# Gated attention stage: the projection ahead of the maxima chunk in each unit, at most two chunks to a unit, and the expert ranks one operation at a time

## The reference, cut to what matters

```
B, T, DIM = (4, 1024, 128);  H, E, DH, K = (8, 5, 64, 3)
ss = sigmoid(x @ Ws).reshape(b, t, H, E);  sd = sigmoid(x @ Wd).reshape(b, t, H, E)
ms, md = topk_mask(ss, K), topk_mask(sd, K)          # 3 of 5 experts stay
q5 = (x @ Wq).reshape(b, t, H, E, DH)                # k5, v5 alike, from Wkv
q = einsum('bthed,bthe->bhtd', q5, sd * md)          # k, v with ss * ms
attn = softmax(einsum('bhid,bhjd->bhij', q * DH**-0.5, k))
out = einsum('bhij,bhjd->bihd', attn, v)
o5 = (out @ Wo).reshape(b, t, H, E, DIM)
y = einsum('bthem,bthe->btm', o5, md)
x = layernorm(x + y)
```

## Time and profile before

| what | value |
|---|---|
| median of three runs | 4347.36 us (4346.91 to 4350.75) |
| the profiled execution's own time | 4350.9 us |
| its span in the profile | 4349.2 us |
| gated stage, unit 0 of group 0 to the end of group 15's products | 1280 to 2529 us |
| mean granted TensorE clock over the span | 0.955 |
| busy shares of the span | PE 89%, DVE 75%, POOL 68%, ACT 44% |

### The profile page before, as it was taken

One profiled execution on the slowest core, in us unless ns is written; L12 is line 12 of the kernel. 1 busy time (PEld: TensorE's weight loads), 2 busy tenths in 40 slices (PEclk: granted clock), 3 DMA queues, 4 the chain that ended last, 5 costly groups with the idle time before them and its releaser, 6 DMA issues. The chain is left out here.

```text
span 4349.2 us, 63343 instructions
## 1 busy us (share of the span) xinstructions
PE 3864.7 (89%) x22554; PEld 2205.7 (51%) x22554; DVE 3243.0 (75%) x5670; ACT 1925.3 (44%) x3478; POOL 2938.9 (68%) x2166
## 2 busy tenths in 40 slices
PE   7999999999788889899899848999999999999964
PEld 4555555555455555555555424555455444545533
DVE  6876878868487777877876648887888788878826
ACT  3443444434355455455455313444444444434423
POOL 3776767667536777877787835777677677767740
PEclk8999999999889999999999968999999999999987
DMA  3000100000010000100100021221222121212121
GB/s 55 21 22 1 38 14 25 10 6 1 27 59 20 28 19 28 38 19 28 33 28 10 6 59 30 41 34 30 39 32 43 30 40 30 43 22 44 19 59 30
DMA packets 98073, 125.90 MB, mean 29 GB/s; under 512 B 28928, under 2 KB 76480, under 8 KB 97760
## 3 DMA queue, kind: packets, MB, share of 16 engines
q1 hardware_dynamic: 97760, 121.86, 13.2%
HBM read 103.69 MB, written 18.12 MB: 28 GB/s over the span
## 5 line engine op out<-in xcount | busy, mean ns | idle before, releaser
L845 POOL TENSOR_TENSOR s_psum_p<-s_psum_p,s_prob 128x1024 f32<-128x1024 f32 (+3 forms) x640 | 1336.9, 2089 | 387.0 <-ACT s_prob L550 336.7
L550 ACT ACTIVATE s_prob<-s_sT 128x1024 f32<-128x1024 f32 (+2 forms) x896 | 792.0, 931 | 842.9 <-DVE s_sT L701 474.1
L449 PE MATMUL s_pv<-s_prob,s_vp 128*64 128x512 f32 (+3 forms) x3584 | 798.9, 567 | 3.9 <-POOL s_prob L830 3.9
L657 DVE CUSTOM_DVE_ANT_0 s_mx<-s_mx,s_strip 128x512 f32<-128x512 f32 x628 | 422.0, 714 | 161.8 <-PE s_mx L406 159.1
L1734 POOL TENSOR_TENSOR s_psum_p<-s_psum_p,s_prob 128x1024 f32<-128x1024 f32 x192 | 462.1, 2407 | 108.0 <-ACT s_prob L1457 106.2
L1457 ACT ACTIVATE s_prob<-s_sT 128x1024 f32<-128x1024 f32 x256 | 262.7, 1026 | 581.5 <-PE s_sT L1321 581.4
L706 DVE RECIPROCAL s_recip<-s_recip 128x128 f32<-128x128 f32 x512 | 452.7, 922 | 34.8 <-ACT s_recip L497 34.8
L406 PE MATMUL s_mx<-s_bh,s_ah 64*128 64x512 f32 (+2 forms) x1756 | 396.7, 447 | 87.2 <-DVE s_bm L647 39.0
L845 POOL TENSOR_TENSOR s_psum_p<-s_prob 128x1024 f32<-128x1024 f32 (+1 forms) x128 | 288.1, 2251 | 204.7 <-ACT s_prob L550 202.0
L449 PEld LDWEIGHTS s_pv<-s_prob,s_vp 128*64 128x64 f32 x3584 | 219.3, 137 | 369.0 <-issue 289.2
L647 DVE TENSOR_REDUCE s_bm<-s_mx 128x6 f32<-128x768 f32 (+2 forms) x376 | 360.0, 957 | 53.3 <-PE s_mx L406 44.6
(11 more groups left out here) (291 smaller groups left out, 7418.7 us busy)
## 6 DMA issues: line engine op xcount, KB each, us to landing
s_strip<-bias_rows SPq DMA_DIRECT2D x256, 144.0 KB, 5.8
s_wr<-gated_weights SPq DMA_DIRECT2D x32, 960.0 KB, 4.9
s_near<-bias_rows SPq DMA_DIRECT2D x256, 48.0 KB, 2.0
x<-s_x SPq DMA_DIRECT2D x10, 512.0 KB, 3.2
s_x<-x SPq DMA_DIRECT2D x8, 512.0 KB, 4.7
gated_weights<-s_side_hi SPq DMA_DIRECT2D x8, 480.0 KB, 2.6
gated_weights<-s_side_lo SPq DMA_DIRECT2D x8, 480.0 KB, 2.9
s_x<-in_L_attn_x_dram SPq DMA_DIRECT2D x4, 512.0 KB, 5.4
```

What stands on the lines that cost most here:

```text
L449: last = mm(pv[heads(hd), lo:CH], vp[:, g % 2, j, heads(hd)], prob[:, k % PR, hd, lo:CH], start=j == 0, stop=end)
L550: nc.scalar.activation(prob[:, k % PR, :, lo:CH], sT[:, k % 2, :, lo:CH], ACT.Exp, scale=st.scale).then_inc(exp_done, 1)
L657: last = nc.vector.tensor_tensor_reduce(out=mx[:, hd, :], in0=mx[:, hd, :], in1=strip[:, g % 2, hd, first:first + CH], scale=1.0, scalar=N ...
L845: nc.gpsimd.tensor_tensor(out[:, :, lo:CH], src, p[:, :, lo:CH], ALU.add)\
```

## The change: what it does

- In each unit PE, and DVE with it, take the projection steps first and the first maxima chunk after them. Before, the chunk came first.
- `mx_steps` becomes one chunk in units 4 to 9 and two in each of units 10 to 14. All go to the bank pair `mx`; the second of a unit still follows the values product.
- `mt_unit` becomes 15, and the transpose stands right behind that unit's scores, ahead of its small jobs and values. `max_rows` stands first on DVE in unit 15.
- Of the products "zp" for blocks 0 to 3 the places become units 13, 14, 15, 15 (before: 12, 13, 14, 15).
- "gx" and "gl" move from units 6 to 9 to units 12 to 15 of groups 0, 3, 7. The rank operations, before in clusters of three (units 10, 11 and 14 of those groups, and 8, 9 and 11 of groups 1, 4, 8), all move to units 0 to 11 of groups 1, 4, 8, one or two at a time. Only a different cutting of the same 20 instructions is made.
- The layer norm's steps 0 and 1 move from units 13 and 14 to unit 15, steps 2 to 5 from unit 15 and units 2, 3, 6 to units 4, 5, 6, 6, step 6 from 7 to 9.

```diff
@@ class Gated @@
-        self.mx_steps = [0] * 4 + [1] * 6 + [2, 2, 3, 3, 0, 0]
+        self.mt_unit = 15
+        self.mx_steps = [0] * 4 + [1] * 6 + [2] * 5 + [0]
...
-        for i in range(4):
-            out[12 + i].append(("zp", g, i))
+        for i, u in enumerate((13, 14, 15, 15)):
+            out[u].append(("zp", g, i))
...
-            for u, job in ((6, ("gx", gated, 0)), (7, ("gx", gated, 1)), (8, ("gl", gated, 0)),
-                           (9, ("gl", gated, 1)), (10, ("top", gated, 0)), (11, ("top", gated, 1)),
-                           (14, ("top", gated, 2))):
+            for u, job in ((12, ("gx", gated, 0)), (13, ("gx", gated, 1)), (14, ("gl", gated, 0)),
+                           (15, ("gl", gated, 1))):
...
-            for k, u in enumerate((8, 9, 11)):
-                out[u].append(("top", ranked, 3 + k))
+            for n, u in enumerate((0, 0, 1, 2, 3, 4, 4, 5, 5, 6, 6, 7, 7, 8, 9, 11)):
+                out[u].append(("top", ranked, n))
...
-        for n, (of, u) in enumerate(((1, 13), (1, 14), (1, 15), (2, 2), (2, 3), (2, 6), (2, 7))):
+        for n, (of, u) in enumerate(((1, 15), (1, 15), (2, 4), (2, 5), (2, 6), (2, 6), (2, 9))):
@@ PE's loop over the units @@
-                early = 1 if steps else 2
-                for t in chunks[:early]:
-                    maxima(t[1], t[2], second(todo, t, k))
+                early = 1
+                if ("mt", g + 1) in todo:
+                    m_transpose(g + 1)
                 for n, t in enumerate(steps):
                     project(t[1], t[2], k if n == 0 else None)
+                for t in chunks[:early]:
+                    maxima(t[1], t[2])
...
                 for t in chunks[early:]:
                     maxima(t[1], t[2])
-                if ("mt", g + 1) in todo:
-                    m_transpose(g + 1)
@@ DVE's loop over the units @@
-                early = chunks[:1] if steps else chunks[:2]
-                for t in early:
-                    maxima(t[1], t[2], second(todo, t, k))
+                early = chunks[:1]
+                if ("mt", g + 1) in todo:
+                    max_rows(g + 1)
                 for n, t in enumerate(steps):
                     project(t[1], t[2], k if n == 0 else None)
+                for t in early:
+                    maxima(t[1], t[2])
```

More of the change, by code:

```diff
@@ L54 @@
 RINGP = 5
-TOPS, TOPC = E0 + 1, 8 + 3 * (E0 - 1)
+TOPS, TOPC = 4 + 3 * (E0 - 1), 8 + 3 * (E0 - 1)
 class Pairs:
@@ L1576, in x_lo, with top_experts @@
                 tt(xl[:, half(c)], xT[:, half(c)], f32(xh[:, half(c)]), ALU.subtract).then_inc(xl_done, 1)
-            def top_experts(b, k):
+            def top_experts(b, n):
                 gates, kept = gate[:, b % 2, :, :], keep[:, :, :]
-                at = TOPC * b + E0 + 3 * (k - 1)
-                if k == 0:
+                k, part = divmod(n + 2, 3)
+                if n == 0:
                     dve.wait_ge(sig_done, 2 * b + 2)
@@ L1585, in top_experts @@
                         nc.vector.memset(kept[:, e, :], float(E0 - 1 - e)).then_inc(top_step, 1)
-                elif k < E0:
+                    return
+                dve.wait_ge(top_step, TOPC * b + E0 + n - 1)
+                if k < E0:
                     later, earlier, won = slice(k, E0), slice(0, E0 - k), beats[:, 0:E0 - k, :]
-                    dve.wait_ge(top_step, at)
-                    tt(won, gates[:, earlier, :], gates[:, later, :], ALU.is_ge).then_inc(top_step, 1)
-                    dve.wait_ge(top_step, at + 1)
-                    tt(kept[:, later, :], kept[:, later, :], won, ALU.add).then_inc(top_step, 1)
-                    dve.wait_ge(top_step, at + 2)
-                    tt(kept[:, earlier, :], kept[:, earlier, :], won, ALU.subtract).then_inc(top_step, 1)
-                else:
-                    dve.wait_ge(top_step, at)
-                    nc.vector.tensor_scalar(kept, kept, float(TOP) - 0.5, None, ALU.is_lt)\
-                        .then_inc(top_step, 1)
-                    dve.wait_ge(top_step, at + 1)
-                    tt(gates, gates, kept, ALU.mult).then_inc(top_step, 1)
+                    if part == 0:
+                        ins = tt(won, gates[:, earlier, :], gates[:, later, :], ALU.is_ge)
+                    elif part == 1:
+                        ins = tt(kept[:, later, :], kept[:, later, :], won, ALU.add)
+                    else:
+                        ins = tt(kept[:, earlier, :], kept[:, earlier, :], won, ALU.subtract)
+                elif part == 0:
+                    ins = nc.vector.tensor_scalar(kept, kept, float(TOP) - 0.5, None, ALU.is_lt)
+                elif part == 1:
+                    ins = tt(gates, gates, kept, ALU.mult)
+                else:
                     if b >= 2:
                         dve.wait_ge(share_done, 2 * NP * (b - 1))
-                    nc.vector.tensor_copy(
+                    ins = nc.vector.tensor_copy(
                         keep_d[:, b % 2, :, :, :],
-                        kept.rearrange("p e (i s h) -> p e i s h", i=NB, s=2)[:, :, :, 1, :])\
-                        .then_inc(top_step, 1)
+                        kept.rearrange("p e (i s h) -> p e i s h", i=NB, s=2)[:, :, :, 1, :])
+                ins.then_inc(top_step, 1)
+                if n == TOPS - 1:
                     dve.wait_ge(top_step, TOPC * (b + 1))
@@ L1696, in _ @@
                             head_maxima(t[1])
-                    elif t[0] == "mt":
-                        max_rows(t[1])
                     elif t[0] == "ln":
```

## The result

The changed kernel took 4379.28 us in the median of five runs (4377.75 to 4382.35), the kernel before, on the same chip, 4348.33 us (4346.91 to 4362.53). The ratio of the two kernels over all these runs is 1.0066, with a 95% interval from 1.0053 to 1.0080: slower by some 29 us (the medians are 31 us apart), where +12 us, 4359 us, had been forecast.

What follows compares the result with a forecast made beforehand. PE was taken to bound the stage, with stalls at bank reads, chunk reductions and rank operations. Terms -15 + 16 + 20 + 19 - 40 - 2 + 14 = +12 on 4347.4 gave 4359 us, range 4328 to 4380.

Steps and rivals of the forecast that it cites:

- the ranks stay dear: Rival: rank operations meet POOL additions as often in their new places, saving only 22 us; 4377 us, chance 0.16.
- term A: Units 4, 6, 7, 8, 9: projection first shortens each period by 0.22 us, -15 us in all.
- term D: Unit 0 of the next group: late products meet POOL additions, so PE waits up to 1.85 us; +19 us.
- term G: Granted clock: the 13 new unit 0 waits bring ten falls of 1.4 us each; +14 us.
- term E: Ranking groups: rank operations spread out remove 40 of their 45.4 us excess over plain groups; -40 us.
- F: Layer norm steps and xs in their new places, against their cost in groups 6 and 10; -2 us.
- term B: Units 10 and 11: the first chunk's reduction stands behind DVE's pieces, units take 6.4 and 6.65 us; +16 us.
- C: Units 12 to 15: all chunks in mx, two turns a unit, and a later transpose lengthen them; +20 us.
- unit 0 doesn't wait: Rival: the late products escape POOL's additions, so unit 0's wait and most clock falls are gone; 4326 us, chance 0.24.
- The waits come, the clock holds: Rival: unit 0 waits as forecast but no clock falls follow; 4345 us, chance 0.20.

Runs made afterwards that it cites:

- run 2: Kernel before with only the new places of the rank operations, gx, gl and layer norm steps: 4304.74 us, ratio 0.9878.
- run 6: The whole change, with the softmax-sum products over 64 columns of ones instead of one: 4361.68 us, ratio 1.0024.
- run 2b: The same kernel as run 2, measured again on another chip: 4307.55 us, ratio 0.9899.
- 3: Kernel before with only at most two chunks a unit, all in mx, transpose in unit 15, products in units 13, 14, 15, 15: 4386.21 us, ratio 1.0061.
- 9: Kernel before with the new rank, gx, gl and layer norm places, and projection first only in units 6 to 9: 4300.36 us, ratio 0.9883.
- 9b: The same kernel as 9, measured again: 4299.69 us, ratio 0.9880.
- 1: Kernel before with only the projection ahead of the chunk in the one-chunk units, 4 to 9: 4356.33 us, ratio 1.0004.
- 4: Kernel before with new rank, gx, gl and layer norm places, and projection first in units 4 to 9: 4308.17 us, ratio 0.9889.
- run 5: The whole change, with the zp products of blocks 0 to 3 moved earlier, to units 12, 12, 13, 14: 4373.02 us, ratio 1.0049.
- Run 11: Kernel before with new rank and layer norm places, projection first in units 10 and 11 too, three chunks kept in units 12 and 13: 4342.45 us, ratio 0.9974.
- 7: Kernel before with new rank and layer norm places, projection first in units 4 to 9, softmax sums over 64 columns: 4304.20 us, ratio 0.9891.
- run 12: Kernel before with new rank and layer norm places, projection first only in units 6 to 9, softmax sums over 64 columns: 4302.26 us, ratio 0.9889.

## Why the forecast was right, and where not

The sign and nearly every unit time held. The range held by luck as much as by reason: 4379.28 us lies 0.7 us inside its upper end, 4380, and outside the 4350 to 4370 that the forecast had for itself. The number nearest to the result, 4377, belonged to the rival that the ranks stay dear, which the runs rule out. The sum, +12, missed the +29 of the ratio by 17 us. Two more errors cancel: term A gained 8 us less than forecast, and term D cost 7 us less. What is left of the miss is nearly all in term G. Term by term, the change against the mean of both profiles of run 2 for all but E and F (table of groups 0 to 13; where falls blur a term, run 6's row, which has the fewest, stands in):

| term | forecast | measured | from |
|---|---|---|---|
| A, projection first | -15 | -7 | run 6: units 6-9 -10.3, units 4-5 +3.6 |
| B, units 10 and 11 | +16 | +15.9, one fall in it | 181.0 against 165.1 |
| C, units 12 to 15 | +20 | +23.6, four falls in it | run 6: 223.2 against 199.6 |
| D, unit 0 | +19 | +12 | 95.3 against 83.3 |
| E and F, ranks, layer norm | -42 | -40 | run 2 against before |
| G, clock | +14 | about +28 | what is left of +28.2 in groups 0 to 13, with C at 19; 22 falls at 1.33 us, from run 6, are 29 |

In the last line the four falls are taken out of C at a good 1 us each, as in unit 12 of the change, 4.82 us with a fall and 3.8 without one. Groups 14 and 15, which the sum had left out, took 107.8 us to the start of their last unit, against 101.8; two profiles of one kernel, runs 2 and 2b, differ there by 3.0 us, so I give no cause for those 6.

**Term G is the step that failed.** The sum let the clock fall only behind the waits of term D: "The 13 new waits of term D would bring ten" falls. Seven of the waits came in full (unit 0 of 7.2 to 8.9 us), and three falls followed. In before, eight of ten such waits had one behind them (two of the ten are in group 14, whose units have no projections, so that six of eight is what the rows give for groups 0 to 13). And in the change there were 22 falls in groups 0 to 13: eleven in units 5 and 6, seven in unit 12, three in unit 1 and one in unit 11. What the sum had left at nothing, or in its upper bound alone, were two other places.

The larger one is units 5 and 6. No wait stands ahead of these eleven falls. In groups 1 to 13 of the change PE has no idle time at all in units 4 and 5, where it had some 0.4 us or more in unit 4 before. Run 6 has as little idle time there and no such fall, so that alone isn't it. Two things go with these falls, in groups 0 to 13:

| unit 5 | profiles | falls in units 5 and 6 |
|---|---|---|
| chunk first, one-column sums | before, 2, 2b, 3, 9, 9b | 1, 0, 1, 0, 0, 0 |
| projection first, one-column sums | the change, 1, 4, 5, 11 | 11, 7, 3, 7, 8 |
| projection first, sums of 64 columns | 6, 7 | 0, 0 |

With both the new order of unit 5 and the one-column products there are 36 falls in five profiles. Where either is missing (run 12, with neither, has none) there are two in nine. The smaller place is unit 12: four of its seven falls (groups 2, 3, 7 and 11) begin behind the new wait of 1.8 us in unit 11, which term B brings and for which the sum had no fall. In run 6, with the same waits, groups 3 and 11 still have theirs.

The price was right: 16 falls fewer made run 6 21.3 us shorter than the change in groups 0 to 13, 1.33 us for each, where 1.4 was taken. The counting was wrong in a second way. Nine of the eleven falls of before began in the six groups with rank operations, and with the ranks' new places run 2 has none in all and run 2b one; the cost of the nine was already in the 45.4 us excess that term E cut from. So nearly all 22 had to be counted as new, not 11 more than before.

**Term A** is right in units 6 to 9 (0.19 us a unit, 0.22 forecast; unit 7 of groups 5, 9 and 13 lost 0.4), half right in unit 4 (4.67 against 4.79 us), and wrong in a sentence that was not priced: "Units 0 to 3 and 5 are full of PE work." Unit 5 is, and there the order costs, 5.94 against 5.55 us. The rows of PE in unit 5, group 11, before:

```profile
2205.97 0.43 PE L1321 MATMUL s_sT<-s_mr,s_rowsel 64*128 64x512 f32 x2
2206.20 0.42 PE L1286 MATMUL s_mx<-s_bh,s_ah 64*128 64x512 f32 x2
2206.55 0.47 PE L1254 MATMUL s_sT<-s_wr,s_xh 128*128 128x448 f32 x1
...
2207.74 0.39 PE L1256 MATMUL s_sT<-s_wr,s_xh 128*128 128x512 f32 x1
2207.97 1.84 PE L1181 MATMUL s_misc<-constants,s_psum_p 128*128 128x1 f32 x16
2209.74 1.08 PE L1333 MATMUL s_pv<-s_prob,s_qkv 128*64 128x512 f32 x4
```

And after:

```profile
2219.04 0.40 PE L1321 MATMUL s_sT<-s_mr,s_rowsel 64*128 64x512 f32 x2
2219.37 0.47 PE L1254 MATMUL s_sT<-s_wr,s_xh 128*128 128x448 f32 x1
...
2220.54 0.40 PE L1256 MATMUL s_sT<-s_wr,s_xh 128*128 128x512 f32 x1
2220.87 0.50 PE L1286 MATMUL s_mx<-s_bh,s_ah 64*128 64x512 f32 x2
2221.30 1.95 PE L1181 MATMUL s_misc<-constants,s_psum_p 128*128 128x1 f32 x16
2223.17 1.08 PE L1333 MATMUL s_pv<-s_prob,s_qkv 128*64 128x512 f32 x4
```

The same products take 3.77 us in the one order (2205.97 to 2209.74) and 4.13 in the other. A chunk is a pair of 64-row products, as the scores are, and follows them after 0.23 us. Between 128-row products it starts 0.33 after the last of them, and the next starts 0.43 after it. The Trainium skill ("TensorEngine Tiling (Array Packing)", section "Key Properties") says that a change of the tiling mode drains the engine. The rows agree: the new order has one such change more in each direction. No run varies this alone.

**Terms B and C** had the right mechanism and size, worked out from one turn in `mx`. Run 11 shows that B would have cost 31 us in units 10 to 15, falls in unit 12 included, and not 16, had the three chunks stayed in units 12 and 13: with two chunks there part of B's cost isn't paid. The terms were not independent, and the sum took them as if they were.

**Term D** is shown by the rows above and by run 5, which takes 17.2 us from unit 0. Against run 2 it is 12 us and not 19. The seven full waits are there, 1.9 to 2.1 us each (in groups 6 and 10 on top of one for the layer norm, 8.9 us against 7.0). The six shorter ones, 6.3 us of the forecast, are not: unit 0 of groups 5, 9 and 13 has 5.46 us against 5.37, and groups 1, 4 and 8, which already waited there in run 2 (6.6 us), wait less in the change (5.4, 6.0, 6.0).

**Terms E and F** were right within 2 us by the profiles, on the reading that the excess of the ranking groups is nearly all stall; whole executions gained 44 and 51 us, so they are known to some 10 us only.

Of the rivals, "unit 0 doesn't wait" and "the ranks stay dear" fell by the rows. "The waits come, the clock holds" is half true: it held after most of those waits, and fell elsewhere. Still open is what decides in which group a fall comes. In the change unit 6 is slowed in group 11 (6.06 us) and not in group 9 (4.53 us) behind the same work of PE in unit 5, and in the old order of unit 5 the same products brought a fall in group 2 of before and in group 8 of run 2b, and none in four other profiles. Not tried was the change with wide sums and early products together.

## What to carry to other kernels

Value a change of order at the engine that is full, too, and not only at the wait that it shortens: use it only in the units where that wait exists (here four of eight, worth 7.9 us, with a loss of 4 us in two others and of 16 in the last two). Price the parts of a packed schedule together, for a reduction that comes late in one unit is paid by the next. Before counting clock falls as caused by idle time, list each fall with the unit in which it begins, and look at what PE did ahead of it, not only whether it was busy.

## What the runs showed of the hardware

- A clock fall behind a stretch without idle time: PE busy 5.94 us of 5.94, then a mean granted clock of 0.72. Sixteen products of one column are in that stretch, and the profile shows them as busy time. With 64 columns each, 2.00 us instead of 1.95 for the sixteen, the eleven falls in units 5 and 6 were gone; with the chunk first in unit 5 and one column, six profiles have two such falls in all. The Trainium skill ("TensorE: Matmul & The Clock Gate", Part 1) has the clock follow how busy PE has been of late. The falls behind waits agree with that; this one, behind a stretch that the profile shows as busy throughout, would not be read from it.
- A chunk of two 64-row products costs some 0.36 us more between 128-row products than beside other 64-row ones (4.13 against 3.77 us for the same products of unit 5).
- The comparing and counting rank operations on DVE took up to 2754 ns in clusters, as POOL's additions ran beside them, and at most 869 ns one at a time.
